# A decoder layer on one core: the first loads reordered, one statistics chain for each of the first four tiles, and transposes of the identity ahead of the work

## The reference

```python
x = x + attn(layernorm(x), Wqkv, bqkv, Wo, bo)        # one head of width 256
x = x + matmul(fake_quant(layernorm(x)), fake_quant(ctx))
x = x + ffn(layernorm(x))

def attn(x, Wqkv, bqkv, Wo, bo):
    qkv = x @ Wqkv + bqkv                              # (2, 512, 3 * 256)
    q, k, v = three slices of 256
    return softmax(q @ k.T / 16) @ v @ Wo + bo

def fake_quant(x, s, z):
    return (clip(round(x / s + z), 0, 255) - z) * s

def ffn(x):                                            # 3584 hidden units, blocks of 64
    inter = x @ c1.T @ c2.T
    idx = the argmax of each block of 64
    h = relu(w1[idx] . x)
    return h @ w2t[idx]
```

## Time and profile before

| | |
|---|---|
| three runs | 858.01, 853.85, 857.35 us; median 857.35 |
| the profiled execution | 854.2 us; its span, first to last instruction, 852.4 us |
| TensorE busy | 816.6 us, 96% of the span |
| VectorE, ScalarE, GpSimd busy | 524.0, 232.7 and 251.4 us (61%, 27%, 29%) |
| chain that ended last | PE 81%, DVE 15%, ACT 1%, DMA 1%, issue 1% |
| TensorE's first instruction | 11.21 us into the span |
| DMA | 53.20 MB, mean 62 GB/s; 8.03 MB of it in the first 40 us |

### The profile page before, as it was taken

How to read it: one execution, slowest core, us unless ns; L and a number is a source line. 1 busy time by engine, 2 the same in 40 slices (tenths; PEclk the granted TensorE clock), 3 DMA queues, 4 the chain that set the end, 5 groups by cost and what they waited for, 6 DMA issues and landing times.

```text
span 852.4 us, 10818 instructions
## 1 busy us (share of the span) xinstructions
PE 816.6 (96%) x3932; PEld 658.4 (77%) x3932; DVE 524.0 (61%) x812; ACT 232.7 (27%) x324; POOL 251.4 (29%) x120
## 2 busy tenths in 40 slices
PE   4999997889899999999999999999999999999998
PEld 4888975447678788878888888878887888778886
DVE  4855799999967852577237832784258624882222
ACT  5366535763320132012201221023102120123100
POOL 2844388515520233013401142024201340124100
PEclk9999999999999999999999999999999999999999
DMA  9126401001210123001210121011200220002022
GB/s 338 38 85 210 151 1 53 1 13 63 99 50 12 32 69 99 12 25 61 87 36 0 49 98 49 12 49 54 93 12 25 74 98 0 25 26 97 0 99 99
DMA packets 16791, 53.20 MB, mean 62 GB/s; under 512 B 3200, under 2 KB 3456, under 8 KB 16640
## 3 DMA queue, kind: packets, MB, share of 16 engines
q1 hardware_dynamic: 16624, 51.85, 17.9%
q10 hardware_dynamic: 144, 1.05, 0.3%
HBM read 48.70 MB, written 4.19 MB: 62 GB/s over the span
## 4 chain that ended last, share of the span: by engine, by line
PE 81%; DVE 15%; ACT 1%; DMA 1%; issue 1%; POOL 0%; SPq 0%; DVEq 0%
PE bank L1187 14%; PE bank L1189 14%; PE bank L1188 14%; PE bank L1368 12%; PE bank L1370 12%; PE bank L1369 12%; DVE stats L797 2%; PE bank L1344 1%; DVE x L910 1%; PE bank L1333 1%; DVE xT_lo L823 1%; DVE pick L960 1%; DVE xn L889 1%; DMA W_raw<-wqkv 1%; DVE cand L953 1%; DVE pairs L1051 1%
## 5 line engine op out<-in xcount | busy, mean ns | idle before, releaser
L471 POOL TENSOR_TENSOR w_lo<-w_raw,w_hi 128x1024 fp32r<-128x1024 f32 x56 | 141.1, 2535 | 471.2 <-ACT w_hi L600 471.2
L1368 PE MATMUL bank<-w_hi,h_hi 128*128 128x512 f32 x448 | 177.6, 396 | 0.0
L1187 PE MATMUL bank<-xT_hi,w_hi 128*128 128x512 f32 x448 | 175.8, 392 | 0.0
L1370 PE MATMUL bank<-w_hi,h_lo 128*128 128x512 f32 x448 | 174.7, 390 | 0.0
L1369 PE MATMUL bank<-w_lo,h_hi 128*128 128x512 f32 x448 | 174.6, 390 | 0.0
L1189 PE MATMUL bank<-xT_hi,w_lo 128*128 128x512 f32 x448 | 174.5, 390 | 0.0
L1188 PE MATMUL bank<-xT_lo,w_hi 128*128 128x512 f32 x448 | 174.5, 389 | 0.0
L968 DVE SCALAR_TENSOR_TENSOR bank<-bank,maskT 128x512 f32<-128x512 f32 x56 | 39.0, 699 | 154.5 <-PE bank L1189 153.3
L983 DVE TENSOR_TENSOR x<-bank,x 128x512 f32<-128x512 f32 x112 | 76.9, 688 | 76.4 <-PE bank L1370 75.0
L607 ACT ACTIVATE maskT<-bank 128x512 bf16<-128x512 bf16 x56 | 33.4, 597 | 290.8 <-PE bank L1344 290.8
L1370 PEld LDWEIGHTS bank<-w_hi,h_lo 128*128 128x128 f32 x448 | 84.1, 188 | 17.7
(11 more groups left out here) (140 smaller groups left out, 969.4 us busy)
## 6 DMA issues: line engine op xcount, KB each, us to landing
w_raw<-w SPq DMA_DIRECT2D x56, 512.0 KB, 3.3
x<-x_in SPq DMA_DIRECT2D x8, 512.0 KB, 10.5
ctx_raw<-ctx_in SPq DMA_DIRECT2D x8, 512.0 KB, 3.9
xn<-ctx_in SPq DMA_DIRECT2D x8, 512.0 KB, 4.8
out<-x SPq DMA_DIRECT2D x7, 512.0 KB, 2.6
W_raw<-wqkv SPq DMA_DIRECT2D x6, 512.0 KB, 10.4
c_raw<-c SPq DMA_DIRECT2D x56, 32.0 KB, 1.8
Wo_raw<-wo ACTq DMA_DIRECT2D x1, 1024.0 KB, 4.8
```

The costliest lines, as they stand in the source:

```text
L471: nc.gpsimd.tensor_tensor(lo, raw, hi.bitcast(F32), ALU.subtract).then_inc(w_lo_done, 1)
L1187: nc.tensor.matmul(dst, ah, bh, start=n == 0, stop=False)
L1368: nc.tensor.matmul(dst, h_hi[:, j, m], w2_hi[:, j, c], start=j == 0, stop=False)
L1370: last = nc.tensor.matmul(dst, h_lo[:, j, m], w2_hi[:, j, c], start=False, stop=j == GJ - 1)
```

## The change

* TensorE, before its first work: 40 transposes of the identity matrix into PSUM bank 7, as soon as the identity is there (`WARM = 40`).
* SyncE: the same loads in the order x0, V's first half, x1, V's second half, x2, x3, the two halves of Q, three biases, x4, x5, the two halves of K, x6, x7. The weight's access pattern is written with k and d merged into one dimension of 1024.
* `CHAINS`: tiles 0, 1, 2 and 3 have a square root and a `norm_scale` each.
* V's second half gets its high part on VectorE (`tensor_copy`) instead of ScalarE, with a semaphore of its own (`V_hi_done`), for which GpSimd's second `W_lo` waits.
* ScalarE and VectorE: the order around it, below.

```diff
-CHAINS = [(0, 0, 2), (0, 2, 2), (0, 4, 4), (1, 0, 4), ...
+CHAINS = [(0, 0, 1), (0, 1, 1), (0, 2, 1), (0, 3, 1), (0, 4, 4), (1, 0, 4), ...
...
-            def load_W(i):
-                for h in range(2):
+            def load_W(i, *halves):
+                for h in halves:
                     k = slice(h * KD // 2, (h + 1) * KD // 2)
-                    sp.dma_start(W_raw[:, i, k, :], wqkv[i][:, k, :]).then_inc(W_loaded[i][h], 16)
-
-            load_x(0, 1)
-            load_W(W_ORDER[0])
+                    sp.dma_start(W_raw[:, i, k, :].rearrange("p k d -> p (k d)"),
+                                 wqkv[i][:, k, :].rearrange("p k d -> p (k d)")).then_inc(W_loaded[i][h], 16)
+
+            load_x(0)
+            load_W(W_ORDER[0], 0)
+            load_x(1)
+            load_W(W_ORDER[0], 1)
             load_x(2, 3)
+            load_W(W_ORDER[1], 0, 1)
             ...
-            load_W(W_ORDER[1])
             load_x(4, 5)
-            load_W(W_ORDER[2])
+            load_W(W_ORDER[2], 0, 1)
             load_x(6, 7)
...
             for n, i in enumerate(W_ORDER):
                 for h in range(2):
-                    pool.wait_ge(W_hi_done, 2 * n + h + 1)
+                    if (n, h) == (0, 1):
+                        pool.wait_ge(V_hi_done, 1)
+                    else:
+                        pool.wait_ge(W_hi_done, 2 * n + (h + 1 if n == 0 else h))
...
             roots(0, 0)
             hi_W(W_ORDER[0], 0)
             norm(0, 0)
+            roots(0, 1)
+            both(hi_T, 0, 0)
             norm(0, 1)
-            hi_W(W_ORDER[0], 1)
-            both(hi_T, 0, 0)
+            roots(0, 2)
             both(hi_T, 0, 1)
-            roots(0, 2)
             norm(0, 2)
+            roots(0, 3)
             norm(0, 3)
             both(hi_T, 0, 2)
             both(hi_W, W_ORDER[1])
...
-            first_stats(0, 1)
+            first_stats(0)
             norm_scale(0, 0)
-            first_stats(2, 3)
+            first_stats(1)
+            dve.wait_ge(W_loaded[W_ORDER[0]][1], 16)
+            nc.vector.tensor_copy(W_hi[:, W_ORDER[0], KD // 2:KD, :],
+                                  W_raw[:, W_ORDER[0], KD // 2:KD, :]).then_inc(V_hi_done, 1)
+            norm_scale(0, 1)
             lo_T(0, 0)
+            first_stats(2)
             norm_scale(0, 2)
             lo_T(0, 1)
+            first_stats(3)
+            norm_scale(0, 3)
             dve.wait_ge(bias_loaded, 48)
             lo_T(0, 2)
...
             pe.wait_ge(ident_ready, 1)
+            for i in range(WARM):
+                nc.tensor.transpose(bank[7][:, (i % 4) * P:(i % 4 + 1) * P], id_f[:, :], id_f[:, :])
             transpose_norm(0, 0)
```

More of the change, by code:

```diff
@@ L30 @@
 EPS = 1e-5
+WARM = 40
 ROUND = 12582912.0
@@ L66 @@
 HIDDEN = [(0, 0), (0, 1), (1, 0), (1, 1), (2, 0), (3, 0), (2, 1), (3, 1)]
-CHAINS = [(0, 0, 2), (0, 2, 2), (0, 4, 4), (1, 0, 4), (1, 4, 2), (1, 6, 2), (2, 0, 4), (2, 4, 2), (2, 6, 2)]
+CHAINS = [(0, 0, 1), (0, 1, 1), (0, 2, 1), (0, 3, 1), (0, 4, 4), (1, 0, 4), (1, 4, 2), (1, 6, 2), (2, 0, 4), (2, 4, 2), (2, 6, 2)]
 W_ORDER = (2, 0, 1)
@@ L255, in decoder_layer @@
         W_hi_done = sem("W_hi_done")
+        V_hi_done = sem("V_hi_done")
         W_lo_done = sem("W_lo_done")
```

## The result

| | before | changed |
|---|---|---|
| 15 executions each, median | 855.33 us (852.14 to 858.29) | 857.32 us (856.82 to 860.33) |
| ratio | | 1.0044, 95% interval 1.003 to 1.0057 |
| profiled execution, time and span | 854.2, 852.4 | 857.2, 855.4 |
| TensorE's wait for the normalised tile, in all | 14.9 us | 10.7 us |
| tile 4's transposes start | 43.26 | 45.50 |

The change makes the kernel slower by 0.44%, about 3.8 us, by the ratio with its interval. The executions spread by 6 us before and by 3.5 after, so the size depends on how it is taken: the medians are 2.0 us apart, the means (855.4 and 858.1) 2.8. All of these lie within the 0.5% that the prediction counts as no change. The time forecast, 859, is 1.7 above the median measured; the shift forecast, +3.0, lies among the three.

A forecast was written before the change was run, and what follows sets the result against it. Bound: tile 4 waits for eight GpSimd instructions, set by when ScalarE rounds the first Q half. Its move from 21.70 to 24.7 gives +3.0 us: 857.2 profiled, 859 from the mean 855.9; range 855 to 862.5.

The forecast's parts named there:

- the shift forecast: Whole kernel: Q half, GpSimd's queue and tile 4 move later, +3.0 us; chance 0.55.
- the Q half: Start of ScalarE's rounding of the first Q weight half; forecast to move from 21.70 to 24.7 us.
- the sum: Up to tile 4: Q half and eight GpSimd instructions later, tile 4's transposes 43.26 to 46.3; everything behind relative to TensorE.
- Loads: At the start, slow rate (221 GB/s between 5 and 5.5 us) returns: V half at 7.60, tile 1 at 8.88.
- 4 KB rows: Weight loads: the weight goes in 4 KB rows already, so the merged access pattern is worth nothing.
- Chains: VectorE, tile 1: copy ends 0.54 after GpSimd, a chain instruction is caught by GpSimd's second V part, chain's last at 14.55.
- Tile 4: VectorE reaches the chain of tiles 4 to 7 about 37.4, is caught by GpSimd; tile 4's transposes at 46.3.
- Warm-up: TensorE's start: at most 1.4 us, counted as nothing since the wait for tile 4 does not move with it.
- The rule on transposes: TensorE's clock: the skill says transposes do not count as busy, so the warm-up gives nothing in any case.
- Full-rate loads: Rival at the start: loads run at 418 GB/s, V half rounded at 5.9; +1.2 us, 857; chance 0.2.
- The free chain: Rival on VectorE: tile 1's chain is not caught; with full-rate loads -1.7 us, 854.2; chance 0.1.
- The clock lost in the gap ahead of tile 4: Rival on TensorE: longer idling costs the clock, 1.4 us again behind tile 4; +4.4 us, 860.3; chance 0.1.

The follow-up runs named there:

- e0: Kernel before with only the weight's access pattern merged into 4 KB rows; ratio to before 1.0015 (0.9997 to 1.0032).
- e4: Kernel before with GpSimd's additions of bo held until the chain of tiles 4 to 7 is done; ratio to before 0.9971.
- e5: e4 with 60 transposes of the identity ahead of tile 0; ratio to before 0.9982.
- e2: Changed kernel with the old load order (x0, x1, both V halves, x2, x3, then as changed), six executions; ratio to before 1.0080.
- e11: e5 with 18 more transposes of the identity between tile 1's transposes and the V projection; ratio to before 0.9978.
- e3: Changed kernel with GpSimd's second V subtraction also waiting until the chain of tile 1 is done; ratio to before 1.0029.
- e1: Changed kernel without the 40 warm-up transposes of the identity; ratio to before 1.0039.
- e8: Kernel before with only the loads in the new order, one chain still serving tiles 0 and 1; ratio to before 0.9994.

## Why the prediction was right, and where it was not

*The shift from before.* Direction and place were right: the change moves the Q half, and the whole of GpSimd's queue and tile 4 with it. That the +3.0 and the 857.2 for the profiled execution came out to the tenth is luck. At tile 4 the shift is 2.2, not 3.0, and the missing 0.8 arises near 235, where the sum had nothing ("Behind tile 4 everything is relative to TensorE"). Over the executions the medians are 2.0 apart.

*Loads.* V half at 7.09 (7.60 forecast), x1 at 8.39 (8.88). The weak stretch returned (213 GB/s at 5 us) but cost 0.5 us less. All later steps up to the Q half are early by this 0.5: tile 1's chain at 13.99 (14.55), the Q half at 24.16 (24.7). The forecast took one landing for the landing. With the old order of loads the V half is rounded at 8.88 in the profile of before, 8.97 in e0, but 7.85 in e4, 8.03 in e5, 8.28 in e2 and 8.61 in e11; with the new order and a chain for each tile, at 6.73 to 7.09. (512 KB at 418 GB/s is 1.25 us, not 1.28.)

*4 KB rows.* Nothing, shown by e0 and by an unchanged packet line. (Of the 1922 packets 1920 are under 8 KB, 3024 less 1104, and that is the fifteen transfers exactly; the two others are not of them.)

*Chains.* The copy ended 0.56 behind GpSimd (0.54), one instruction of tile 1's chain held to the end of the second subtraction: as forecast, and shown to be the cause of the late Q half by e3, in which GpSimd's second subtraction alone is moved and the Q half returns to 21.76.

*Tile 4.* VectorE came to the chain of tiles 4 to 7 at 36.25, not 37.4, and was caught all the same. 45.50 against 46.3: 0.5 from the loads, the rest since the caught last instruction ends right at GpSimd's end, where before it started behind it.

*Warm-up, the step that failed.* That it is worth nothing in the changed kernel was right (e1). The reason was half wrong: "those 1.4 us lie ahead of the wait for tile 4, which does not move with them". That holds for the changed kernel, where ScalarE's and VectorE's chains set the Q half. It does not hold for the kernel before. The row at 20.73 in the earlier trace rows says so: ScalarE waits 1.67 us for TensorE there. With the clock up early (e0) before's tile 4 starts at 41.90, and against that the change loses 3.6 us, not the 2.2 of the two profiles. So the sum, made against a profiled execution of the late sort, does not hold against the others: the price of the change is smaller or larger with the sort. How the 15 executions of before split by the time of the first rise was not recorded, and the measured size is itself uncertain (2.0 to 3.8 us by the way it is taken), so whether this term moved the total is open.

*The rule on transposes.* The Trainium skill ("TensorE: Matmul & The Clock Gate", PE-mode transpose) had them not counting for the clock, and I wrote that the trace agrees as far as it goes. It does not: 40 transposes and nothing else brought the clock to 2.4 GHz at 6.1 us here, in e4 the transposes of tiles 0 and 1 from 10.19 on did so by 13.0, and in e0 those from 11.30 on by 14.7. In the trace of before, the same sixteen were followed by slow matmuls until 19.0; that one trace could not settle it.

*The rivals.* Full-rate loads: no. The free chain: no, e3 shows what it would have been. The clock lost in the gap ahead of tile 4: not in the changed kernel's profile, but in e3's and e8's (idle 2.80 and 2.01 us). I gave it 0.1 as something on top. The six executions of the changed kernel at 0.992, 2.0 us slower than the nine, would fit it, but equally one near 110.

## What to carry to other kernels

A tiny VectorE instruction with two operands in SBUF that meets a GpSimd instruction on whole tiles lasted here until that one was through (2.3 us instead of 0.16), and in a chain each one can be caught anew. Place such a chain where GpSimd is idle, or let GpSimd wait for it, which is a single semaphore wait. Holding the additions of bo in this way is the only edit here that made the kernel faster than before (e4, 0.9971). Moving a step to another engine so that its end starts a long GpSimd instruction just ahead of such a chain cost more here than it gave (e3 took 2.4 us back). And before counting a gain at TensorE, look at which engine waits for TensorE between there and the next stall: if none does, the gain ends there, as e1 shows. If one does, as in the kernel before, the gain can be part of the spread of its executions already.

## What the hardware did that I had not expected

* fp32 transposes of the identity raise TensorE's clock (above), and a clock that is up can be lost behind short idle times: 2.35 us (e5), 2.01 (e8), 2.80 (e3), 1.88 (e0, near 110) and 2.28 (e11, near 146), each time 0.3 to 1.2 us after work had begun again. The same idle time does not always lose it: 2.78 us in the changed kernel's profile did not, nor did 1.86 in before's, near 111.
* The same 3.4 us at half clock near 235 cost nothing in e1 and e8. What goes with a loss there, in all fourteen profiles, is that `pick` meets GpSimd's subtraction and not `cand`.
* The same instructions in two executions differ by 1.4 us at tile 4 (43.26 and 41.90) through the time at which the clock rose, and by 3.1 us in what follows (809.1 and 812.2), 0.6 of it near 110 and 2.4 near 235. In a kernel of 855 us whose effect to be measured is 3, one profiled execution of each is not enough to read a difference from.
